# Rounded key and value products, rows of 2 KB, another first norm and new orders in a cross-attention and expert layer

## What is computed

```python
Q = norm(x) @ Wq.T + bq;  K = ctx @ Wk.T + bk;  V = ctx @ Wv.T + bv   # 16 heads of 16
x = x + softmax(Q K^T / 4) V @ Wo.T + bo
s = softmax(norm(x) @ G);  w = s kept for its two largest, else 0
h = silu(norm(x) @ gate_w) * (norm(x) @ up_w)
x = x + sum_e w_e (h_e @ down_w_e) + sum_e w_e (norm(x) @ lora_A_e) @ lora_B_e
```

## Time and profile before

| | |
|---|---|
| time of the profiled execution | 112.87 us |
| its span in the trace | 111.1 us |
| median of three runs | 112.47 us |
| TensorE busy | 105.6 us |
| VectorE busy | 91.2 us |
| ScalarE busy | 68.3 us |
| GpSimd busy | 48.6 us |

### The profile page before, as it was taken

How to read it: one execution, slowest core, us unless ns; L and a number is a source line. 1 busy time by engine, 2 the same in 40 slices (tenths; PEclk the granted TensorE clock), 3 DMA queues, 4 the chain that set the end, 5 groups by cost and what they waited for, 6 DMA issues and landing times.

```text
span 111.1 us, 2549 instructions
## 1 busy us (share of the span) xinstructions
PE 105.6 (95%) x884; PEld 81.3 (73%) x884; DVE 91.2 (82%) x193; ACT 68.3 (61%) x120; POOL 48.6 (44%) x76
## 2 busy tenths in 40 slices
PE   6999999899999998999999999999999999999990
PEld 6987868677767565877666677768756898888960
DVE  5528288979997899899799997999889978889940
ACT  0064462669998986584899668869494822733210
POOL 6359876970697594000660440040735056560000
PEclk9999999999999999999999999999999999999999
DMA  2994769979924004070200000000000000002043
GB/s 39 365 369 174 282 165 335 366 280 271 368 77 184 10 3 189 28 264 6 94 6 3 0 0 3 0 6 3 0 6 0 0 0 0 6 3 94 3 165 118
DMA packets 9372, 11.90 MB, mean 107 GB/s; under 512 B 976, under 2 KB 6416, under 8 KB 9360
## 3 DMA queue, kind: packets, MB, share of 16 engines
q1 hardware_dynamic: 8656, 11.22, 29.1%
q10 hardware_dynamic: 704, 0.53, 1.4%
HBM read 4.34 MB, written 1.05 MB: 48 GB/s over the span
## 4 chain that ended last, share of the span: by engine, by line
PE 77%; ACT 5%; DVE 5%; DMA 3%; issue 3%; SPq 2%; POOL 1%; ACTq 1%; POOLq 0%
PE unit L761 25%; PE unit L768 16%; PE unit L863 10%; PE unit L850 8%; PE unit L831 7%; PE unit L773 5%; PE unit L787 3%; DMA xs<-x 3%; ACT probs L584 2%; ACT xn L537 2%; PE unit L894 2%; PE unit L837 2%; SPq L337 2%; ACTq L337 1%; DVE rowmax L682 1%
## 5 line engine op out<-in xcount | busy, mean ns | idle before, releaser
L682 DVE TENSOR_REDUCE rowmax<-unit 128x4 f32<-128x1024 f32 x32 | 37.7, 1212 | 3.5 <-PE unit L831 3.5
L584 ACT ACTIVATE probs<-unit 128x1024 f32<-128x1024 f32 x32 | 32.0, 1025 | 9.1 <-PE unit L850 9.0
L863 PE MATMUL unit<-probs,vaug 128*32 128x256 f32 x256 | 15.7, 382 | 0.0
L831 PE MATMUL unit<-kstack,qstack 63*128 63x256 f32 x128 | 13.4, 304 | 0.6 <-ACT probs L584 0.3
L850 PE MATMUL unit<-qstack,kstack 64*128 64x256 f32 x128 | 13.5, 302 | 0.4 <-DVE rowmax L682 0.4
L850 PEld LDWEIGHTS unit<-qstack,kstack 64*128 64x128 f32 x128 | 9.4, 185 | 5.1 <-issue 2.8
L831 PEld LDWEIGHTS unit<-kstack,qstack 63*128 63x128 f32 x128 | 9.4, 185 | 5.0 <-issue 2.3
L487 POOL TENSOR_TENSOR x2T_lo<-x2T,x2T_hi 128x512 fp32r<-128x512 f32 x4 | 5.1, 1286 | 17.5 <-ACT x2T L549 11.4
L863 PEld LDWEIGHTS unit<-probs,vaug 128*32 128x32 f32 x256 | 7.4, 109 | 5.2 <-ACT probs L584 0.4
L453 POOL TENSOR_SCALAR vare<-mv 128x2 f32<-128x2 f32 x8 | 1.8, 221 | 19.8 <-DVE mv L628 19.7
L761 PE MATMUL unit<-xT,wa 128*128 128x256 f32 x32 | 7.9, 391 | 0.1
(11 more groups left out here) (106 smaller groups left out, 212.1 us busy)
## 6 DMA issues: line engine op xcount, KB each, us to landing
kstack<-k_hi SPq DMA_DIRECT2D x8, 256.0 KB, 2.7
qstack<-q_hi SPq DMA_DIRECT2D x6, 256.0 KB, 3.0
cT<-ctxT SPq DMA_DIRECT2D x4, 256.0 KB, 3.7
kstack<-k_lo SPq DMA_DIRECT2D x4, 256.0 KB, 3.1
out<-xs SPq DMA_DIRECT2D x8, 128.0 KB, 1.8
wa<-wattn SPq DMA_DIRECT2D x3, 256.0 KB, 4.4
xs<-x SPq DMA_DIRECT2D x3, 256.0 KB, 3.2
qstack<-q_lo SPq DMA_DIRECT2D x3, 256.0 KB, 2.6
```

Source lines behind the costliest of these rows:

```text
L584: act.activation(probs[:, n % NPAIR], unit[PAIR[name, n] // 2][:], ACT.Exp, scale=SCALE).then_inc(exp_done, 1)
L682: dve.tensor_reduce(rowmax[:, b % 2, :, i // 4, :, i % 4].rearrange("p t j -> p j t"), unit[PAIR[name, n] // 2][:], AX.X, ALU.max)\
L831: ins = pe.matmul(dst[:, j, t], qs[rows, PLACE[i], t * P:(t + 1) * P], ks[rows, PLACE[i]], start=True, stop=True)
L863: ins = pe.matmul(dst[QUAD * j:QUAD * (j + 1), i], vaug[:, of % 3, t, 4 * g + j], probs[:, n % NPAIR, j % 2, t], start=(t == 0), stop=(t = ...
```

## The change

- Loads: the arrays lie in memory so that each partition's part is one row of 2 KB (wf 5 KB); the same bytes.
- wk and the biases go first, on ScalarE's queue; x:0 moves to the sync queue behind c:0. The order of the other loads and of the stacking DMAs changes.
- First norm: batch 0's deviation by ScalarE's square root (`root`), a reciprocal on VectorE, and the two halves of the tokens on VectorE and ScalarE at once (`shift1`, `norm1:0`, `n1h`). Two new activations on a scratch value, `table` and `table2`, load ScalarE's tables for the root and for the exponential.
- Keys and values of batches 2 and 3 in rounded parts: `wkhi`, `wvhi`, `chi` on ScalarE, `wklo`, `wvlo`, `clo` on GpSimd, twelve rounded matmuls of 256 columns instead of four plain ones. The parts use tiles of the expert layer that are idle then, so `chi:3` waits for batch 2's products, and `outshi`, `x2T:1` and the first `hl` for batch 3's.
- The bias step: VectorE multiplies wo's rows with bv and adds the two halves (`bprod`), and one product with ones sums the rows, instead of two products.
- The warm-up has 8 products on a constant instead of 11, without a wait for a memset.
- All five orders are new; among much else v:2 and v:3 come earlier, wf is loaded later, the down weights earlier.

```diff
-NWARM = 11
+NWARM = 8
...
+CONTEXT_PARTS = [2, 3]
...
 ORDERS = {
     "tensor": """
-        k:0@0 xT:0@1 bias:0@2 qh:0@1 qh:1@0 k:1@2 v:0@1 max:0.0@4 xT:1@0 max:0.1@2 max:0.2@6 max:0.3@4 q:1@0
-        v:1@1 max:0.4@2 max:0.5@6 mrow:0.0@4 xT:2@5 k:2@0 max:0.6@2 max:0.7@4 attn:0.0@6 q:2@1 max:1.0@2
-        max:1.1@4 attn:0.1@6 k:3@0 max:1.2@2 mrow:0.1@1 attn:0.2@4 max:1.3@6 xT:3@1 max:1.4@2 attn:0.3@4
-        max:1.5@6 q:3@1 max:1.6@2 max:1.7@4 attn:0.4@6 u:0.0@0 mrow:1.0@1 attn:0.5@2 max:2.0@6 attn:0.6@4
-        u:0.1@0 attn:0.7@2 max:2.1@6 attn:1.0@4 u:1.0@1 u:1.1@1 max:2.2@2 attn:1.1@4 attn:1.2@6 mrow:1.1@0
-        v:2@1 max:2.3@4 max:2.4@6 attn:1.3@2 o:0@0 attn:1.4@2 max:2.5@4 max:2.6@6 mrow:2.0@1 v:3@0 attn:1.5@4
-        attn:1.6@2 max:2.7@6 u:2.0@1 u:2.1@1 attn:1.7@2 max:3.0@4 attn:2.0@6 u:3.0@0 u:3.1@0 attn:2.1@2
-        max:3.1@6 mrow:2.1@1 attn:2.2@4 max:3.2@2 x2T:0@0 o:1@1 attn:2.3@4 max:3.3@6 attn:2.4@2 u:4.0@0
-        u:4.1@0 attn:2.5@2 attn:2.6@4 max:3.4@6 mrow:3.0@1 low:0@0 glu0:0@2 max:3.5@0 max:3.6@4 attn:2.7@6
-        glu1:0@3 x2T:1@0 max:3.7@6 attn:3.0@4 u:5.0@1 u:5.1@1 attn:3.1@2 attn:3.2@4 attn:3.3@6 mrow:3.1@0
-        low:1@1 glu0:1@0 o:2@1 attn:3.4@2 attn:3.5@4 attn:3.6@6 u:6.0@0 attn:3.7@2 hl:0@1 u:6.1@0 u:7.0@4
-        u:7.1@4 glu1:1@0 hl:1@2 hl:2@3 x2T:2@4 o:3@5 down:0@1 low:2@0 glu0:2@2 down:1@3 x2T:3@0 glu1:2@1
-        hl:3@4 low:3@0 down:2@2 glu0:3@5 hl:4@4 hl:5@0 down:3@1 glu1:3@3 down:4@4 hl:6@0 down:5@5 hl:7@0
-        down:6@3 down:7@2
+        k:0@0 xT:0@1 qh:0@1 qh:1@0 k:1@2 v:0@1 max:0.0@4 max:0.1@6 max:0.2@2 xT:1@0 v:1@1 max:0.3@4 max:0.4@6
+        q:1@0 mrow:0.0@1 k:2@2 max:0.5@4 max:0.6@6 v:2@1 max:0.7@2 attn:0.0@4 xT:2@0 bias:0@1 attn:0.1@6
+        attn:0.2@4 max:1.0@2 mrow:0.1@0 q:2@1 max:1.1@2 max:1.2@6 attn:0.3@4 k:3@0 max:1.3@2 max:1.4@4
+        attn:0.4@6 u:0.0@1 max:1.5@2 mrow:1.0@0 attn:0.5@6 max:1.6@4 u:0.1@1 attn:0.6@2 xT:3@0 attn:0.7@4
+        max:1.7@6 u:1.0@1 attn:1.0@2 max:2.0@4 u:1.1@1 max:2.1@6 attn:1.1@2 attn:1.2@4 q:3@0 mrow:1.1@1
+        max:2.2@2 max:2.3@4 attn:1.3@6 v:3@1 max:2.4@2 max:2.5@6 mrow:2.0@4 o:0@5 max:2.6@0 attn:1.4@2
+        attn:1.5@6 u:2.0@4 max:2.7@2 attn:1.6@0 u:2.1@4 attn:1.7@6 attn:2.0@0 max:3.0@2 u:3.0@5 u:3.1@5
+        attn:2.1@0 max:3.1@6 attn:2.2@2 mrow:2.1@4 x2T:0@5 max:3.2@0 u:4.0@4 low:0@5 max:3.3@2 attn:2.3@6
+        max:3.4@0 o:1@5 mrow:3.0@2 attn:2.4@6 max:3.5@0 attn:2.5@2 u:4.1@4 max:3.6@6 attn:2.6@0 attn:2.7@2
+        glu0:0@5 attn:3.0@0 max:3.7@6 attn:3.1@2 u:5.0@4 u:5.1@4 attn:3.2@0 attn:3.3@6 x2T:1@2 mrow:3.1@3
+        glu1:0@4 low:1@2 o:2@3 attn:3.4@0 attn:3.5@6 u:6.0@2 attn:3.6@4 attn:3.7@0 hl:0@3 u:6.1@2 u:7.0@4
+        u:7.1@4 x2T:2@2 hl:1@5 glu0:1@0 low:2@1 o:3@2 down:0@3 hl:2@0 glu1:1@1 glu0:2@2 down:1@3 x2T:3@1
+        hl:3@4 glu1:2@5 low:3@1 hl:4@0 down:2@2 glu0:3@1 hl:5@4 down:3@2 glu1:3@3 down:4@5 hl:6@4 down:5@0
+        hl:7@1 down:6@3 down:7@2
     """,
     "scalar": """
-        x:0 biases k:0 xT:0 qh:0 qhih:0 qh:1 k:1 norm1:1 xT:1 v:0 q:1 norm1:2 mrow:0.0 wfhi:0 xT:2 v:1 k:2
-        attn:0.0 q:2 attn:0.1 norm1:3 mrow:0.1 attn:0.2 xT:3 k:3 attn:0.3 q:3 attn:0.4 mrow:1.0 attn:0.5-7
-        attn:1.0-1 mrow:1.1 attn:1.2-3 v:2 outshi mrow:2.0 attn:1.4-6 v:3 attn:1.7 attn:2.0 norm2:0 attn:2.1
-        mrow:2.1 attn:2.2 x2T:0 attn:2.3-6 mrow:3.0 low:0 norm2:1 exps:0 attn:2.7 glu0:0 glu1:0 x2T:1
-        attn:3.0-1 mrow:3.1 attn:3.2 low:1 attn:3.3 glu0:1 attn:3.4 exps:1 attn:3.5-7 norm2:2 hl:0 glu1:1
-        hl:1 x2T:2 hl:2 low:2 exps:2 glu0:2 x2T:3 glu1:2 hl:3 low:3 exps:3 glu0:3 hl:4 hl:5 glu1:3 hl:6 hl:7
+        wk biases table:0 wkhi root:0 n1h:0 k:0 xT:0 qh:0 qhih:0 qh:1 k:1 norm1:1 v:0 table2:0 chi:2 xT:1
+        wvhi v:1 q:1 mrow:0.0 k:2 norm1:2 v:2 attn:0.0 xT:2 attn:0.1 chi:3 mrow:0.1 attn:0.2 q:2 attn:0.3 k:3
+        attn:0.4 norm1:3 mrow:1.0 attn:0.5-7 attn:1.0 xT:3 outshi attn:1.1-2 mrow:1.1 wfhi:0 attn:1.3 q:3
+        mrow:2.0 v:3 attn:1.4-7 attn:2.0 norm2:0 attn:2.1 mrow:2.1 x2T:0 attn:2.2 low:0 attn:2.3 mrow:3.0
+        attn:2.4-7 norm2:1 attn:3.0-1 exps:0 glu0:0 x2T:1 mrow:3.1 attn:3.2 glu1:0 low:1 attn:3.3 exps:1
+        attn:3.4-7 norm2:2 x2T:2 hl:0 hl:1 glu0:1 low:2 glu1:1 hl:2 glu0:2 exps:2 x2T:3 hl:3 glu1:2 low:3
+        hl:4 exps:3 glu0:3 hl:5 glu1:3 hl:6 hl:7
     """,
     "vector": """
-        minus:0 ln1:0 norm1:0 k:0 ln1:1 bias:0 qh:0 qh:1 k:1 max:0.0-1 ln1:2 max:0.2-3 q:1 max:0.4-7 ln1:3
-        max:1.0-7 max:2.0 u:0 max:2.1 u:1 max:2.2-4 o:0 max:2.5-6 ln2:0 max:2.7 u:2 max:3.0 u:3 max:3.1-2 o:1
-        ln2:1 max:3.3 u:4 max:3.4 route1:0 max:3.5-6 glu0:0 glu1:0 max:3.7 u:5 route2:0 route3:0 route1:1
-        glu0:1 o:2 route2:1 route3:1 ln2:2 u:6 u:7 hl:0 hl:1 glu1:1 o:3 ln2:3 hl:2 down:0 route1:2 norm2:3
-        route2:2 route3:2 glu0:2 glu1:2 route1:3 hl:3 route2:3 down:1 route3:3 glu0:3 hl:4 weigh:6 hl:5
-        glu1:3 weigh:7 down:2 down:3 down:5 down:6 down:4 down:7
+        minus:0 ln1:0 shift1:0 norm1:0 ln1:1 k:0 qh:0 bprod:0 qh:1 k:1 max:0.0-3 ln1:2 max:0.4 q:1 max:0.5-7
+        bias:0 max:1.0 ln1:3 max:1.1-6 u:0 max:1.7 max:2.0-1 u:1 max:2.2-5 o:0 max:2.6 ln2:0 max:2.7 u:2
+        max:3.0 u:3 max:3.1-4 o:1 max:3.5 ln2:1 route1:0 max:3.6 u:4 max:3.7 u:5 route2:0 route3:0 glu0:0
+        route1:1 glu1:0 o:2 ln2:2 route2:1 route3:1 u:6 u:7 hl:0 glu0:1 route1:2 hl:1 route2:2 o:3 ln2:3
+        down:0 glu1:1 norm2:3 glu0:2 route3:2 hl:2 hl:3 glu1:2 route1:3 route2:3 down:2 route3:3 down:1
+        glu0:3 hl:4 hl:5 weigh:6 glu1:3 weigh:7 down:3 down:5 down:4 down:6 down:7
     """,
     "gpsimd": """
-        consts ones ln1:0 zero:0 minus:1 ln1:1 xo:0 xo:1 zero:1 ln1:2 minus:2 zero:2 ln1:3 k:2 xo:2 q:2 k:3
-        q:3 wflo:0 xo:3 ln2:0 outslo x2T:0 ln2:1 x2T:1 weigh:0 weigh:1 weigh:2 ln2:2 x2T:2 ln2:3 weigh:3
-        x2T:3 weigh:4 weigh:5
+        ones wklo consts zero:0 ln1:1 minus:1 zero:2 minus:2 clo:2 wvlo zero:1 ln1:2 xo:0 clo:3 k:2 ln1:3 q:2
+        xo:1 xo:2 k:3 outslo q:3 xo:3 ln2:0 wflo:0 x2T:0 ln2:1 x2T:1 weigh:0 ln2:2 weigh:1 x2T:2 weigh:2
+        ln2:3 weigh:3 weigh:4 x2T:3 weigh:5
     """,
     "sync": """
-        c:0 wk wq wv wo x:1 c:1 obias khi:0 klo:0 qloh:0 qhih:1 qloh:1 x:2 khi:1 klo:1 c:2 wf qhi:1
-        mstack:0.0 qlo:1 x:3 c:3 outs khi:2 qhi:2 mstack:0.1 klo:2 qlo:2 mstack:1.0 khi:3 mstack:1.1 qhi:3
-        klo:3 mstack:2.0 qlo:3 mstack:2.1 mstack:3.0 mstack:3.1 out:1 out:0 out:3 out:2 out:5 out:6 out:4
+        c:0 x:0 wq c:1 x:1 wo obias wv khi:0 klo:0 qloh:0 qloh:1 c:2 qhih:1 khi:1 x:2 klo:1 x:3 outs
+        mstack:0.0 qhi:1 qlo:1 c:3 mstack:0.1 khi:2 qhi:2 klo:2 wf qlo:2 mstack:1.0 khi:3 klo:3 mstack:1.1
+        qhi:3 mstack:2.0 qlo:3 mstack:2.1 mstack:3.0 mstack:3.1 out:2 out:1 out:3 out:5 out:4 out:0 out:6
         out:7
     """,
 }
...
+        c_hi, c_lo = (part[:].rearrange("p t k s -> p (t k s)")[:, 0:KT * T].rearrange("p (k t) -> p k t", k=KT)
+                      for part in (hlT_hi, hlT_lo))
+        wk_hi, wk_lo = wd_hi[:], wd_lo[:]
+        wv_hi, wv_lo = x2T_hi[:, 1], x2T_lo[:, 1]
+        eps, scratch = sb("eps", [P, 1]), sb("scratch", [P, 1])
+        deviation = sb("deviation", [P, ST])
+
+        bias_rows = hid[:, 0, 0]
...
         def load_x(engine, b):
-            engine.dma_start(xs[:, b], x[b].rearrange("(t p) d -> p t d", p=P)).then_inc(x_in[b], 16)
+            engine.dma_start(xs[:, b], x[b]).then_inc(x_in[b], 16)
 
         def load_context(engine, b):
-            engine.dma_start(cT[:, b], ctxT[b].rearrange("(k p) t -> p k t", p=P)).then_inc(c_in[b], 16)
+            engine.dma_start(cT[:, b], ctxT[b]).then_inc(c_in[b], 16)
 
         def load_weights(engine, name):
-            n, at = WEIGHTS[name]
-            view = wattn.rearrange("(k p) o -> p k o", p=P)
-            engine.dma_start(wa[:, :, at], view[:, :, at]).then_inc((wk_in, wq_in, wv_in)[n], 16)
+            n = WEIGHTS[name]
+            engine.dma_start(wa[:, n], wattn[n]).then_inc((wk_in, wq_in, wv_in)[n], 16)
...
+                if name in ("wklo", "wvlo"):
+                    w = name[0:2]
+                    hi, lo = (wk_hi, wk_lo) if w == "wk" else (wv_hi, wv_lo)
+                    pool.wait_ge(w_hi_ready[w], 1)
+                    pool.tensor_tensor(lo, wa[:, WEIGHTS[w]], hi.bitcast(F32), ALU.subtract).then_inc(w_parts[w], 1)
+                    pool.wait_ge(w_parts[w], 1)
+                if name == "clo":
+                    n = CONTEXT_PARTS.index(b) + 1
+                    pool.wait_ge(c_hi_ready, n)
+                    pool.tensor_tensor(c_lo, cT[:, b], c_hi.bitcast(F32), ALU.subtract).then_inc(c_parts, 1)
+                    pool.wait_ge(c_parts, n)
...
+                if name == "table":
+
+                    act.wait_ge(eps_ready, 1)
+                    act.activation(scratch[:], eps[:], ACT.Sqrt).then_inc(tables, 1)
+                if name == "table2":
+                    act.wait_ge(tables, 1)
+                    act.activation(scratch[:], eps[:], ACT.Exp).then_inc(tables, 1)
```

(65 more changed lines are left out.)

59 lines of the change are left out of this document (38 added, 21 removed).

## The result

| | before | changed |
|---|---|---|
| median of the runs | 112.56 us (112.32 to 112.91, 4 runs) | 116.52 us (115.23 to 116.85, 4 runs) |
| ratio, 95% interval | 1 | 1.029 (1.024 to 1.034) |

A forecast was written before the change was run, and what follows sets the result against it. Bound by TensorE, VectorE close behind. 1.75 us ahead near 30 us, less a 0.4 us wait, leaves 1.35, the rest even: profiled 112.87 becomes 111.5, median 0.4 lower, 111.1 us; range 110.3 to 112.0.

The forecast's parts named there:

- The start: Loads, warm-up and first norm: qh:0 starts at 9.1 instead of 9.31 us, gain 0.2 us (0.5 lost to 0.6 gained).
- The new wait: On ScalarE chi:2, ahead of xT:1, waits for c:2 until 17.0 to 17.3 us; q:1 at 18.6, 0.5 us lost.
- The two rivals here: On ScalarE: late contexts, 113.7 us, chance 0.17; second table load holding it 1.28 us more, 111.5 us, chance 0.07.
- The rounded parts: TensorE's keys and values of batches 2 and 3: 1.43 instead of 1.73 us each, 1.2 us less in all.
- max:1.0 and VectorE: zero:1 holds qhi:1 and max:1.0 to about 26.4 us, VectorE not there before 26.7; max:1.1 done about 31 us.
- For the rest of the run ... even: Behind about 30 us: two extra run starts (0.4 us) against stalls that v:3, k:3 and q:3 fill, nothing net.
- the tail is unchanged: End of the kernel: no gain or loss counted.
- What feeds the parts lies beside: GpSimd's four differences of 1.29 us and ScalarE's four copies of 0.58 us lie beside TensorE's work, in time for it.
- bias on the path: TensorE's bias step falls from 0.87 to 0.43 us but moves behind xT, so it costs 0.43 us on the path.
- VectorE becomes the bound: Rival: VectorE has 1.3 us more work, TensorE waits for maxima, gain shrinks to about 0.3 us: 112.2 us, chance 0.13.
- Its sign: Sign that the forecast is wrong: VectorE idles less than 3 us after 30 us while TensorE waits for it.
- The slower rival: ScalarE: c:2 lands at 18.9 instead of 17.3 us, 1.6 us added, c:3 about 1 more: 113.7 us, chance 0.17.

The follow-up runs named there:

- Run 4: Kernel before with only the changed start (2 KB rows, wk on ScalarE's queue, norm by root, eight warm-ups, table loads): 112.42 us, ratio 0.997.
- run 6: Changed kernel with eight unread products of 128 columns put before attn:2.2 to fill TensorE's pause: 115.17 us, ratio 1.016.
- run 5: Changed kernel with wflo:0 before q:3 on GpSimd and plain keys and values for batches 2 and 3: 113.57 us, ratio 1.004.
- run 10: Run 9 with zero:1 ahead of clo:2 and wvlo, and qhi:1, qlo:1 ahead of mstack:0.0 in the sync queue: 114.86 us, ratio 1.018.
- run 8: Run 1 with the fill zero:1 moved ahead of clo:2 and wvlo on GpSimd: 112.95 us, ratio 1.0005.
- run 1: Changed kernel with one word moved, wflo:0 before q:3 on GpSimd instead of behind ln2:0: 112.89 us, ratio 1.002.
- run 9: Run 1 with the transposes x2T:2 behind hl:1 and glu0:1 on TensorE, their copies behind glu0:1 on ScalarE: 114.35 us, ratio 1.012.
- run 2: Kernel before with wflo:0 moved behind ln2:0 on GpSimd: 113.43 us, ratio 1.006.
- run 7: Run 4 with the values of batches 2 and 3 in rounded parts, keys plain: 112.92 us, ratio 0.998 to the kernel before.
- run 11: Changed kernel with wf_lo left in place but computed by two GpSimd instructions instead of one: 114.03 us, ratio 1.009.
- run 3: Changed kernel with plain keys and values for batches 2 and 3, the rounded parts out of the orders: 116.25 us, ratio 1.029.

## Why the prediction was wrong, step by step

**The start: right.** The first product starts at 4.37 us, the first statistics at 4.95 (so the tokens had landed by the 5.1 forecast), the transposes at 7.48 (7.65), qh:0 at 8.83 (9.1), max:0.0 at 14.18 (14.4), each in one trace. From the changed kernel's timeline:

```profile
6.01 0.29 ACT L567 ACTIVATE deviation<-mv,eps 128x2 f32<-128x2 f32 x1 [1.11 <-DVE mv L696]
6.34 0.17 DVE L714 RECIPROCAL rstd<-deviation 128x2 f32<-128x2 f32 x1 [0.36 <-ACT deviation L567]
...
8.83 1.97 PE L844 MATMUL unit<-xT,wa 128*128 128x256 f32 x8 [0.72 <-ACT xT L613]
```

Run 4 gives 0.3 us for all of it; 0.2 were forecast.

**The new wait: right, with some luck.** "The fastest context landed after 3.3 us: 17.0 to 17.3 us" came true to the tenth:

```profile
14.89 1.28 ACT L564 ACT_TABLE_LOAD   x1
16.19 0.20 ACT L564 ACTIVATE scratch<-eps 128x1 f32<-128x1 f32 x1
17.32 0.62 ACT L582 CAST hlT_hi<-cT 128x512 fp32r<-128x512 f32 x1 [0.93 <-DMA cT<-ctxT]
```

q:1 starts at 18.63 (18.6 forecast). The luck lies in what ends ahead of it. c:2 goes out behind VectorE's second q_lo, forecast to end at 13.55 us and ended at 13.63; but bprod, which stands ahead of that, took 2.35 us instead of 0.84, and the input of q_lo was ready from 12.35. In run 6, where bprod escapes a hold by GpSimd (last section), q_lo starts at 12.40 instead of 13.15 and ends at 12.88, c:2 goes out 0.74 us earlier, chi:2 starts at 16.58 without a wait, and q:1 at 18.37. So bprod was not free, as the forecast had it: the walk was 0.7 us too long elsewhere, and the hold made up for it.

The two rivals here fall by the same rows. c:2 isn't late, and chi:3 waits for c:3 only to 28.58 us, where 28.3 was forecast. ScalarE's copy ahead of the second table load ends at 14.88 us, the load starts 0.01 us later, and its end is followed by the next instruction after 0.02: it holds nothing beyond its 1.28 us. The drain of 1.38 us, which the forecast had set beside it from the Trainium skill, "ScalarE: Activation LUTs", section "What ACT_TABLE_LOAD costs", doesn't appear.

**The rounded parts: right on TensorE's list, worth less in the kernel.** "1.2 in all" is 1.2 by the places shown with run 5. The single terms were both short, 1.43 for 1.61 and 1.73 for 1.82 to 1.93, because the pace was taken from the middle of a run and the way in and out of it costs up to 0.2 us; the errors cancel in the difference. What the forecast had wrong is that all of it reaches the end: by the clock of the whole kernel it is 0.24 to 0.87 us.

**max:1.0 and VectorE: wrong.** "zero:1 ... holds qhi:1 in the sync queue and so max:1.0 to about 26.4 us". It starts on TensorE at 28.02:

```profile
26.57 0.88 PE L943 MATMUL unit<-qstack,kstack 64*128 64x256 f32 x8
28.02 0.50 PE L924 MATMUL unit<-kstack,qstack 63*128 63x256 f32 x4 [0.56 <-issue]
```

The sync queue issues batch 1's queries some microseconds before that:

```profile
21.76 0.65 SPq L429 DMA_DIRECT2D qstack<-mT  x1
22.61 1.19 SPq L352 DMA_DIRECT2D qstack<-q_hi  x2
23.90 1.63 SPq L352 DMA_DIRECT2D qstack<-q_lo  x1
```

And the view of the tile q_lo from 23.5 to 28 us, which has that one issue:

```profile
DMA to landing us min/median/max: 4.0/4.0/4.0
```

q_lo goes out at 23.90 us and lands 4.0 later, and max:1.0 starts 0.1 us behind that landing. The same 0.1 us stands between the two in nine of the ten traces with the new orders, with landings from 27.03 to 28.46 us; the tenth is run 10, where q_lo goes out 0.8 us earlier and TensorE arrives after it has landed. So the gate is the last piece of the queries, 1.3 us behind the q_hi that the forecast took, and not the fill (run 8). q:2 is done at 30.5 us instead of 29.4. With the 0.9 us less that it then has to do than the kernel before at 30.24, TensorE stands 0.65 us ahead and not 1.75. VectorE finishes max:1.1 at 32.2, not 31.

**"For the rest of the run ... even": the step that failed.** The forecast put everything behind 30 us at nothing: two more run starts against filled stalls, and "the tail is unchanged". The runs show 3.0 us lost there by the place of one GpSimd instruction (changed kernel against run 1). The new orders otherwise lose 0.8, in part ahead of 30 us, where TensorE's lead was 1.1 us smaller than forecast.

The 3.0 us come from a cost that the sum doesn't have. Behind it stands "What feeds the parts lies beside": I costed GpSimd's work by whether it was done in time for TensorE, and VectorE's by its own durations, and never asked whether the two can run together. For the forms shown in the last section they can't. And I priced only the new differences, not the old one that the diff moves: wflo:0 stands in the diff of GpSimd's order, at 2.39 us the longest instruction of that engine, and no sentence of the forecast names it. The third omission is the clock: it was thought of for the pause before qh:0 and nowhere else, and it made 1.4 of the 3.0 us.

The 0.8 us are what run 5 loses against run 4 by the ratios (1.004 and 0.997, intervals apart); both have plain products, and in neither is the un at 55 us held for long. The new order fills TensorE well from 30 to 80 us (in run 1 it reads 10.00 of every ten). But x2T:2 has to wait 0.65 us at 83.2 us, and in the kernel before the waits of this kind (TensorE for a norm by ScalarE) come to 0.3 us in all. This part isn't taken apart further: run 9 and run 10, which tried its two visible pieces, both made it worse. What of it is bias on the path (0.43 us forecast), what run starts and what the queue stays open.

In a sum, by the ratios: the start 0.3 us gained (run 4), the new orders 0.8 lost (run 5 against 4), the parts 0.24 gained (run 1 against 5), the place of wf_lo 3.0 lost (changed against run 1): 3.3 us lost. It closes on the 1.029 because each step starts where the one before ends; the two small terms are no larger than the intervals of their runs.

Of the rivals, "VectorE becomes the bound" came nearest, with TensorE waiting for a maximum, but by a stretched instruction and not by more work, and at 112.2 us it priced this 4.3 us too low. Its sign, VectorE idle for less than 3 us, did come up (0.9 us from 30 to 60 us, with TensorE idle for 1.86), but run 1 has the same 1.0 us of idle VectorE with TensorE full, so the sign doesn't tell the two apart. The slower rival (ScalarE held by a context) didn't happen.

## What to carry to other kernels

Before an instruction is moved on GpSimd, write down what VectorE does in the stretch where it lands; a TENSOR_TENSOR with two operands in SBUF that starts there is held for what is left of a wide GpSimd difference, so put wide GpSimd work beside maxima and transposes, or cut it into pieces. Price every token that an order moves, not only those that are new. And look at how TensorE's pauses are filled: here one of 1.86 us cost 1.4 us more behind it in five executions of eight, and in two other kernels ones of 0.78 and 0.75 us cost only themselves.

## What the hardware showed that I had not expected

**VectorE held by GpSimd.** Over the traces of all fourteen kernels: TENSOR_TENSOR with both operands in SBUF (un, 0.42 us free) that starts beside a wide GpSimd TENSOR_TENSOR is held and ends 0.28 us behind it, as un shows four times (57.77 and 57.48 us in the changed kernel, 57.51 and 57.23 in run 2, 43.09 and 42.81 in run 7, 57.17 and 56.89 in run 11). `ahead<-ahead,tied` grows from 0.29 to 1.33 us and ends 0.14 us behind:

```profile
77.87 1.27 POOL L519 TENSOR_TENSOR x2T_lo<-x2T,x2T_hi 128x512 fp32r<-128x512 f32 x1 [5.31 <-ACT x2T L613]
77.95 1.33 DVE L805 TENSOR_TENSOR ahead<-ahead,tied 128x128 f32<-128x128 f32 x1
```

Beside GpSimd's rstd, which takes 0.71 us for 128x2 elements, the same instruction takes its 0.29 us: in these traces only wide GpSimd work holds it. TENSOR_SCALAR on f32 in SBUF is held too, even beside a memset. First the changed kernel, then run 6, where VectorE starts 0.10 us before the memset:

```profile
10.76 1.81 POOL L526 MEMSET kstack<- 128x2048 f32 x1
10.88 1.83 DVE L750 TENSOR_SCALAR hid<-wo,bias_sb 128x256 f32<-128x256 f32 x1
12.62 1.83 POOL L529 MEMSET qstack<- 128x2048 f32 x1
12.75 0.48 DVE L751 SCALAR_TENSOR_TENSOR hid<-wo,bias_sb,hid 128x256 f32<-128x256 f32 x1
```

```profile
10.89 0.34 DVE L751 TENSOR_SCALAR hid<-wo,bias_sb 128x256 f32<-128x256 f32 x1
10.99 1.98 POOL L527 MEMSET kstack<- 128x2048 f32 x1
```

So the one that starts second is held: VectorE's takes 0.34 us instead of 1.83, and the memset 1.98 instead of 1.81. bprod, which is these two VectorE instructions, was forecast at twice 0.42 us.

Not held, in any of the traces: the maxima out of PSUM (300 of them beside GpSimd instructions of over 0.5 us, none over 1.23 us), the 32x32 transposes, the statistics, TENSOR_TENSOR with one operand in PSUM, and the SCALAR_TENSOR_TENSOR above with both in SBUF. The Trainium skill, "GPSIMD Engine Reference", section "Specifications", says that GpSimd's way into SBUF is shared with VectorE and that they contend where VectorE's instruction is in a mode that uses two ports or has two inputs in SBUF. un, ahead and the maxima agree. The SCALAR_TENSOR_TENSOR has two inputs in SBUF and takes 0.48 us in ten traces of ten; but it always stands beside a memset, which reads nothing, while every instruction that held un or ahead reads two tiles. Whether its form or its partner lets it escape isn't shown, since no trace has this form, with wide operands in SBUF, beside a GpSimd difference, or un beside a memset.

**The clock behind a pause.** Behind 1.86 us of idle TensorE the granted clock read 0.62 and 0.53 over four microseconds (the changed kernel's rows); by the mean clocks of the single executions it fell in three of four of the changed kernel and in two of four of run 3, and those were 1.2 to 1.6 us longer. Behind 0.78 and 0.75 us it stayed at 1.00 (runs 2 and 11, no mean below 0.996 in 19 executions), and with the pause filled by products that nobody reads it stayed at 1.00 too (run 6, four of four).
